# Moving the first heads' preparations earlier, and an HBM ring 256 KB further on

## The chip, the cores and the metric

The kernel runs on 1 core of one Trainium2 chip. The metric is the device time of one execution in microseconds (us), lower is better. Unprofiled runs give the time; one profiled execution gives the trace.

## The reference

For x of shape (32, 512, 256) in float32 it computes

```python
xn  = _layernorm(x)
out = x + attention(xn) + expert_ffn(xn)
# attention, 16 heads of width 16, relative positions:
content_score = einsum('bhsp,bhtp->bhst', q + u, k)
pos_score     = _relative_shift(einsum('bhsp,htp->bhst', q + v, pos))
weights       = softmax((content_score + pos_score) / sqrt(P))
att           = einsum('bhst,bhtp->bhsp', weights, val) @ Wo + bo
# expert FFN: softmax gate over 8 experts, each expert takes its top k tokens, gelu(x @ w1) @ w2,
# results weighted by the gate and scattered back with add
```

## The kernel before, in words

Three phases follow one another: attention, expert FFN, and the sum with the output projection. The change touches the attention phase alone. Its two stages:

- **The batch loop** (`for b in range(B)`, B = 32, once on each engine). SP loads x of batch b + 4 (L300) once batch b is normalised, stores the normalised batch to `xn_d` (L304) and its transposed form to `xt_d` (L308). DVE computes `statistics(b + 1)` (L616, L619) and `normalise(b)` (L624, L630). TensorE transposes (`turn_batch`, L810) and multiplies by the gate weights (`score(b - 1)`, L819). ACT takes square roots (`find_root`, L479) and evacuates the transposes (`copy_turned`, L486). The order on each engine is the order in which the code is written: each engine runs its own list and meets the others at semaphores.
- **The head loop** (512 heads: 16 turns of `body(i)` with 32 heads each). A head's position scores are made by TensorE (`position`, L907), evacuated by ACT to `xo` (L537), written by SP into one of 8 slots of the ring `xs_d` in HBM (L348, rows of 513 values), and read back one value shifted (L356, rows of 512), which is the relative shift. DVE adds content scores and the shifted scores (L677), ACT takes the exponential (L542), TensorE transposes the weights (L940), DVE and ACT evacuate them (L687, L551), and TensorE multiplies by the values (L956).

Before the head loop can start, the first heads need preparations: GpSimd splits the transposed batch 0 in high and low parts (`split_xt`, L447, L449, after SP's `load_xt(0)`, L313), TensorE projects values, queries and keys (`project_v` L863, `project_q` and `project_k` L846, all into the one PSUM bank `mp`), DVE evacuates the values (`stage_v`, L665), ACT the queries and keys (`keep_queries` L501, `keep_keys` L508), GpSimd splits them (`with_v`, `keys`, `with_u`; L417, L419, L437, L439), and TensorE spreads the queries over partitions (`spread_qv`, L830, L831), which DVE evacuates (`qv_evacuate`, L643). In the kernel before, these steps stand in the turns for batches 27 to 30 of the batch loop and right behind it, and the engine that takes a product out of `mp` does so in the same turn in which TensorE makes it. The ring is allocated as

```python
xs_d = nc.dram_tensor("xs_d", [8, S * (S + 1)], F32).ap()
```

so one slot is 512 x 513 x 4 = 1,050,624 bytes.

Of the kernel before, what the change touches and what calls it, by code (L numbers as in the profile page):

```python
# [9 lines left out]
F32 = mybir.dt.float32  # L10
# [5 lines left out]
P = 128  # L16
D = 256
DC = D // P
B = 32
S = 512  # L20
# [86 lines left out]
def attention_phase(nc, x, gate_w, w, consts, xn_d, xt_d, xs_d, att_d, sums_d, picks, chosen):  # L107
# [17 lines left out]
    with ExitStack() as ctx:  # L125
# [103 lines left out]
        k_kept = m.sem("k_kept")  # L229
# [9 lines left out]
        qv_out = m.sem("qv_out")  # L239
# [55 lines left out]
        with nc.Block() as block:  # L295

            @block.sync
            def _(sp):
                def load_x(b):
                    sp.dma_start(xin[:, b % NS], x[b].rearrange("(p t) d -> p t d", t=TT)).then_inc(x_in[b % NS], 16)  # L300
# [30 lines left out]
                for b in range(B):  # L331
                    store_xn(b)
                    if b + NS < B:
                        load_x(b + NS)
                    if b:
                        store_xt(b - 1)
                    if b == B - 8:
                        sp.wait_ge(xt_stored[0], 16)
                        load_xt(0)
                store_xt(B - 1)  # L340
# [133 lines left out]
            def _(act):  # L474
# [35 lines left out]
                for b in range(B):  # L510
                    find_root(b)
                    if b:
                        copy_turned(b - 1)
                    if b == 3:
                        act.wait_ge(const_in, 16 * CONST_LOADS)
                    if b in (3, 4):
                        keep_positions(b - 3)
                    if b == 5:
                        act.activation(wqkv[:, 0], wst[:, 0:3], ACT.Copy).then_inc(w_high, 1)
                    if 6 <= b < 6 + NG8 // 2:  # L520
                        g = 2 * (b - 6) + 1
                        act.wait_ge(p_spread, g + 1)
                        act.activation(pos[:, g], op[:, :], ACT.Copy).then_inc(p_out_act, 1)
                    if b == B - 3:
                        act.wait_ge(biased, 2)
                        keep_queries(0, 0)
                    if b == B - 2:
                        keep_keys(0, 0)
                copy_turned(B - 1)

# [77 lines left out]
            def _(dve):  # L608
# [29 lines left out]
                def qv_evacuate(i, g):  # L638
                    v = i * GROUPS + g
                    dve.wait_ge(qv_full, v + 1)  # L640

                    wait(dve, x_full, (v - 1) * GH * 2)
                    dve.tensor_copy(qv[:, g % 2], mp[:, :]).then_inc(qv_out, 1)  # L643
# [15 lines left out]
                def stage_v(i, bb, half):  # L659

                    b = i * 2 + bb
                    dve.wait_ge(v_full, b * 2 + half + 1)

                    wait(dve, o_full, (b - 1) * H)
                    dve.tensor_tensor(val[:, bb % 2, 2 * half:2 * half + 2, :, 0:HD],  # L665
                                      mp[:, :].rearrange("p (t h v) -> p t h v", t=2, h=H),
                                      bv[:, :].rearrange("p (h v) -> p h v", h=H).unsqueeze(1).to_broadcast([P, 2, H, HD]),
                                      ALU.add).then_inc(v_ready, 1)
# [46 lines left out]
                for b in range(B):  # L715
                    if b + 1 < B:
                        statistics(b + 1)
                    normalise(b)
                    if b == 2:
                        dve.wait_ge(const_in, 16 * CONST_LOADS)  # L720
                        for k in range(2):
                            dve.tensor_tensor(bias_q[:, k], vectors[:, 0], vectors[:, 3 + k], ALU.add).then_inc(biased, 1)
                    if b in (4, 5):
                        position_lows(b - 4)
                    if b == 6:
                        dve.wait_ge(w_high, 1)
                        dve.tensor_tensor(wqkv[:, 1], wst[:, 0:3], wqkv[:, 0].bitcast(F32), ALU.subtract).then_inc(w_low, 1)
                    if 7 <= b < 7 + NG8 // 2:
                        g = 2 * (b - 7)
                        dve.wait_ge(p_spread, g + 1)  # L730
                        dve.tensor_copy(pos[:, g], mp[:, :]).then_inc(p_out_dve, 1)
                    if b == B - 5:
                        dve.wait_ge(ones_set, 2)
                        stage_v(0, 0, 0)
                    if b == B - 4:
                        stage_v(0, 0, 1)

                qv_evacuate(0, 0)
                qv_evacuate(0, 1)
                qv_evacuate(0, 2)  # L740
                qv_evacuate(0, 3)
                kd_evacuate(0, 0)
# [60 lines left out]
            def _(pe):  # L803
# [9 lines left out]
                def score(b):  # L813

                    pe.wait_ge(copied, b + 1)
                    group, v = b // 4, b % 4
                    of_group = slice(group % 4 * PACK, (group % 4 + 1) * PACK)
                    for c in range(DC):
                        ins = pe.matmul(tp[of_group, group // 4, :], gw[:, c, PACK - NE - v * NE:2 * PACK - NE - v * NE],  # L819
                                        xts[:, b % NS, c, :], start=(v == 0 and c == 0), stop=(v == 3 and c == DC - 1))  # L820
                    ins.then_inc(scored, 1)
# [32 lines left out]
                def project_k(i, t):  # L854
                    project(1, t, k_full)
# [11 lines left out]
                def spread_qv(i, g):  # L867
                    v = i * TILES + g // (MH // GH)
                    pe.wait_ge(qv_high, v + 1)
                    pe.wait_ge(qv_low, v + 1)  # L870
                    spread_out(mp[:, :], QUERIES, g, qc[:, 1, 0], qc[:, 1, 1]).then_inc(qv_full, 1)
# [89 lines left out]
                for b in range(B):  # L961
                    turn_batch(b)
                    if b:
                        score(b - 1)
                    if b == 2:
                        pe.wait_ge(const_in, 16 * CONST_LOADS)
                    if b in (2, 3):
                        project_positions(b - 2)
                    if 6 <= b < 6 + NG8 // 2:
                        pe.wait_ge(p_low, DC)  # L970
                        spread_positions(2 * (b - 6))
                        spread_positions(2 * (b - 6) + 1)
                    if b == B - 5:
                        pe.wait_ge(w_low, 1)
                        pe.wait_ge(xt_low, 1)
                        pe.wait_ge(p_out_dve, NG8 // 2)
                        project_v(0, 0, 0)
                    if b == B - 4:
                        pe.wait_ge(v_ready, 1)
                        project_v(0, 0, 1)  # L980
                    if b == B - 3:
                        pe.wait_ge(v_ready, 2)
                        project_q(0, 0)
                    if b == B - 2:
                        pe.wait_ge(q_kept, 2)
                        project_k(0, 0)
                score(B - 1)
                pe.wait_ge(k_kept, 1)
                spread_qv(0, 0)
                pe.wait_ge(qv_out, 1)  # L990
                spread_qv(0, 1)
                pe.wait_ge(copied, B)
                for k in range(2):
                    for t in range(TT):
# [451 lines left out]
def build(nc, x, Wq, bq, Wk, bk, Wv, bv, Wp, bp, Wo, bo, u, v, gate_w, w1, w2, out):  # L1446
    names = ("sinusoid", "ident", "first_row", "spread")
    c = {n: nc.inline_tensor(a, name=f"const_{n}").ap() for n, a in zip(names, shape_constants())}
    xn_d = nc.dram_tensor("xn_d", [B * S, D], F32).ap()
    xt_d = nc.dram_tensor("xt_d", [B, P, DC, S], F32).ap()  # L1450
    ffn_d = nc.dram_tensor("ffn_d", [B * S, D], F32).ap()
    xs_d = nc.dram_tensor("xs_d", [8, S * (S + 1)], F32).ap()
    att_d = nc.dram_tensor("att_d", [B, D, S], F32).ap()
    sums_d = nc.dram_tensor("sums_d", [B, H, S], F32).ap()
    inv_d = nc.dram_tensor("inv_d", [B, H, S], F32).ap()
    weights = {"Wq": Wq, "Wk": Wk, "Wv": Wv, "Wp": Wp, "bq": bq, "bk": bk, "bv": bv, "bp": bp,
               "u": u.rearrange("a h b p -> (a h b p)"), "v": v.rearrange("a h b p -> (a h b p)")}
    with nc.sbuf_tensor("picks", [P, B * NE], U32) as picks, nc.sbuf_tensor("chosen", [P, B * NE], F32) as chosen:
        attention_phase(nc, x, gate_w, weights, (c["sinusoid"], c["ident"], c["first_row"], c["spread"]), xn_d, xt_d, xs_d,
                        att_d, sums_d, picks, chosen)  # L1460
        ffn_phase(nc, w1, w2, c["ident"], xn_d, picks, chosen, ffn_d, sums_d, inv_d)
    combine_phase(nc, x, Wo, bo, ffn_d, att_d, inv_d, out)
# [27 lines left out]
```

## Time and profile before

| what | value |
|---|---|
| time, median of 3 runs | 5658.08 us (5654.66 to 5665.97) |
| the profiled execution's own time | 5717.12 us |
| its span | 5715.3 us |
| mean granted TensorE clock | 0.936 of full speed |
| PE busy | 5210.5 us, 91% |
| DVE busy | 3630.7 us, 64% |
| ACT busy | 3470.4 us, 61% |
| POOL (GpSimd) busy | 1430.1 us, 25% |
| bytes moved | 1357.75 MB, mean 238 GB/s |

Busy times are sums over a span with different stages: the batch loop fills about the first 187 us, the head loop the time to about 3770 us, FFN and output the rest. PE is TensorE's multiplying, PEld its loading of weights, SP the engine that issues nearly all DMAs. "DMA share" is the mean busy share of the 16 DMA engines.

### The profile page before, as it was taken

The page shows a single profiled execution, that of the slowest core. Times are in us where ns is not written, and L with a number is a line of the kernel's source. Part 1 is how long each engine was busy: PE and PEld are TensorE (multiplying, and loading weights), DVE is VectorE, ACT ScalarE, POOL GpSimd, SP SyncE. Part 2 cuts the span into 40 slices and gives each one's busy share as a digit, 9 for nine tenths or more (in the row PEclk, how much of TensorE's full clock was granted, in tenths as well). Part 3 has the DMA queues.
Part 4 walks back from the last instruction along what each step waited for, and adds up shares of the span by engine and source line. Part 5 has one row for each costly group of instructions (what it writes and reads, how often), then busy time and mean ns, then how long its engine had stood idle before and what let it go on. Part 6 is the DMA issues. An engine that isn't in the chain of part 4 may idle for free. (4 is left out here: it accounts for less than half of the span.)

```text
span 5715.3 us, 126833 instructions
## 1 busy us (share of the span) xinstructions
PE 5210.5 (91%) x42412; PEld 3837.9 (67%) x42412; DVE 3630.7 (64%) x8008; ACT 3470.4 (61%) x5116; POOL 1430.1 (25%) x1032
## 2 busy tenths in 40 slices
PE   6799999999999899999999999979999999999755
PEld 2466666666666666666666666658888988888744
DVE  7598887787777777877777877854333333333233
ACT  2487777787787777777777877844443444344211
POOL 0111111111111111111111111114444444444355
PEclk9799999899899999999998999989999999999877
DMA  9799999999999999999999999983332233222398
GB/s 338 225 327 315 313 311 311 308 317 307 308 317 304 318 307 310 317 305 310 316 304 311 320 306 316 328 272 64 58 59 53 47 58 58 52 49 43 72 289 258
DMA packets 311142, 1357.75 MB, mean 238 GB/s; under 512 B 41792, under 2 KB 119360, under 8 KB 179136
## 3 DMA queue, kind: packets, MB, share of 16 engines
q1 hardware_dynamic: 256704, 1265.12, 69.5%
q0 software_dynamic: 49152, 67.14, 7.2%
q10 hardware_dynamic: 4608, 16.78, 0.8%
q8 instruction: 386, 6.32, 0.5%
q14 instruction: 292, 2.39, 0.1%
HBM read 691.42 MB, written 657.46 MB: 236 GB/s over the span
## 5 line engine op out<-in xcount | busy, mean ns | idle before, releaser
L677 DVE CUSTOM_DVE_ANT_0 att_shifted<-att_quad,att_shifted 128x512 f32<-128x512 f32 x2048 | 1345.4, 685 | 472.2 <-DMA att_shifted<-xs_d 295.2
L537 ACT ACTIVATE att_xo<-att_quad 128x1024 f32<-128x1024 f32 x1024 | 1049.2, 1025 | 720.5 <-PE att_quad L907 718.9
L542 ACT ACTIVATE att_shifted<-att_shifted,att_mn 128x512 f32<-128x512 f32 x2048 | 1359.1, 716 | 83.5 <-issue 75.7
L940 PE MATMUL att_tp<-att_ident,att_shifted 128*128 128x128 f32 x8192 | 1184.8, 290 | 1.0 <-DVE att_pt L687 0.4
L687 DVE COPY att_pt<-att_tp 128x512 f32<-128x512 f32 x1536 | 1014.6, 686 | 208.5 <-PE att_tp L940 207.9
L940 PEld LDWEIGHTS att_tp<-att_ident,att_shifted 128*128 128x128 f32 x8192 | 930.1, 147 | 316.3 <-issue 287.4
L919 PE MATMUL att_quad<-att_kd,att_qu 64*128 64x512 f32 x2048 | 827.5, 472 | 193.5 <-DVE att_mn L677 132.0
L1251 DVE TENSOR_TENSOR ffn_hp<-ffn_hf,ffn_hp 128x512 fp32r<-128x512 f32 x512 | 354.6, 693 | 925.7 <-ACT ffn_hf L1218 925.6
L907 PE MATMUL att_quad<-att_pos,att_qv 64*128 64x512 f32 x2048 | 907.0, 472 | 18.9 <-ACT att_xo L537 18.8
L1216 ACT ACTIVATE ffn_hp<-ffn_up 128x512 fp32r<-128x512 f32 x512 | 306.5, 599 | 926.5 <-PE ffn_up L1308 926.4
L1282 PE MATMUL ffn_yp<-ffn_w2p,ffn_hp 128*128 128x256 f32 x6144 | 831.0, 285 | 29.5 <-DVE ffn_w2p L1259 22.8
L1282 PEld LDWEIGHTS ffn_yp<-ffn_w2p,ffn_hp 128*128 128x128 f32 x6144 | 807.7, 193 | 70.1 <-issue 29.2
L1308 PE MATMUL ffn_up<-ffn_xp,ffn_w1p 128*128 128x512 f32 x3072 | 811.8, 401 | 33.4 <-DVE ffn_w1p L1246 33.4
L919 PEld LDWEIGHTS att_quad<-att_kd,att_qu 64*128 64x128 f32 x2048 | 333.8, 192 | 606.9 <-issue 381.6
L1308 PEld LDWEIGHTS ffn_up<-ffn_xp,ffn_w1p 128*128 128x128 f32 x3072 | 557.5, 194 | 128.4 <-issue 25.4
L1177 POOL DMA_INDIRECT ffn_d<-ffn_ys,picks x256 | 404.4, 1580 | 838.4 <-DVE ffn_ys L1240 824.7
L956 PE MATMUL att_op<-att_pt,att_val 128*17 128x128 f32 x16384 | 592.1, 289 | 0.2 <-issue 0.2
L956 PEld LDWEIGHTS att_op<-att_pt,att_val 128*17 128x17 f32 x16384 | 424.1, 102 | 188.9 <-issue 150.5
L437 POOL CAST att_kc<-att_qn 128x512 fp32r<-128x512 f32 x64 | 39.2, 612 | 1895.9 <-ACT att_qn L508 1895.9
L907 PEld LDWEIGHTS att_quad<-att_pos,att_qv 64*128 64x128 f32 x2048 | 368.4, 193 | 51.4 <-ACT att_xo L537 20.1
L417 POOL CAST att_qc<-att_qn 128x512 fp32r<-128x512 f32 x128 | 144.8, 1132 | 775.2 <-PE att_mp L831 702.6
L551 ACT ACTIVATE att_pt<-att_tp 128x512 f32<-128x512 f32 x512 | 306.3, 598 | 43.2 <-PE att_tp L940 41.7
(108 smaller groups left out, 4992.2 us busy)
## 6 DMA issues: line engine op xcount, KB each, us to landing
xs_d<-att_xo SPq DMA_DIRECT2D x512, 1026.0 KB, 12.1
att_shifted<-xs_d SPq DMA_DIRECT2D x512, 1024.0 KB, 8.9
att_shifted<-in_L_attn_x_dram SPq DMA_DIRECT2D x32, 512.0 KB, 7.5
xn_d<-att_shifted SPq DMA_DIRECT2D x32, 512.0 KB, 6.2
xt_d<-att_shifted SPq DMA_DIRECT2D x32, 512.0 KB, 7.4
att_xf<-xt_d SPq DMA_DIRECT2D x32, 512.0 KB, 9.9
att_d<-att_osb SPq DMA_DIRECT2D x512, 32.0 KB
ffn_d<-ffn_zero SPq DMA_DIRECT2D x8, 2048.0 KB, 24.8
```

The lines of the kernel that those rows point to most:

```text
L537: act.activation(xo[:, kk % NW, 2 * half:2 * half + 2, 1:S + 1], xp[:, :, :], ACT.Copy).then_inc(x_out, 1)
L542: act.activation(shifted[:, kk % NX, t], shifted[:, kk % NX, t], ACT.Exp, bias=mn[:, kk % NX, t:t + 1], scale=-1.0).then_inc(exp_done, 1)
L677: dve.tensor_tensor_reduce(out=shifted[:, kk % NX, t], in0=sp_[:, t % 2], in1=shifted[:, kk % NX, t], scale=-0.25, scalar=-NEG, op0=ALU.ad ...
L687: dve.tensor_copy(pt[:, t], tp[:, t % 2]).then_inc(t_out_dve, 1)
L907: ins = pe.matmul(xp[:, t % 2, :], qv[rows, kk // GH % 2, t * P:(t + 1) * P], pos[rows, kk // GH % NG8, :], start=True, stop=True)
L919: pe.matmul(sp_[:, t % 2, :], qu[rows, kk // GH % 2, t * P:(t + 1) * P], kd[rows, kk // GH % 2, :], start=True, stop=True).then_inc(s_full, 1)
L940: ins = pe.transpose(tp[:, c % 2, t * P:(t + 1) * P], shifted[:, kk % NX, t, c * P:(c + 1) * P], ident[:, :])
L956: ins = pe.matmul(op[32 * t:32 * t + HD + 1, kk % QH * P:(kk % QH + 1) * P], val[:, kk // H % 2, c, kk % H, :], pt[:, c, t * P:(t + 1) * P ...
L1177: pool.indirect_dma_start(ffn_d, bass.IndirectOffsetOnAxis(ap=picks[:, g * GB + k, e:e + 1], axis=0), ys[:, g % 2, k], None, compute_op=AL ...
L1251: dve.tensor_tensor(hp[:, g % 2, 1, f], hf[:, f % 2], hp[:, g % 2, 0, f].bitcast(F32), ALU.subtract).then_inc(h_low, 1)
L1282: ins = pe.matmul(yp[:, k % 2, 0:D], hp[:, g % 2, hi, f, k * CAP:(k + 1) * CAP], w2p[:, wi, f, :], start=(f == 0 and s == 0), stop=(f == F ...
L1308: ins = pe.matmul(up[:, f % 4, :], w1p[:, wi, c, f * P:(f + 1) * P], xp[:, g % 2, xi, c, :], start=(s == 0 and c == 0), stop=(s == 2 and c ...
```

## The change

The preparations of the first heads are spread over the turns 14 to 31 of the batch loop, three turns apart, and each consumer stands two turns behind the product it takes:

| step | turn before | turn now |
|---|---|---|
| `load_xt(0)` on SP | 24 | 8 |
| `project_v(0, 0, 0)` on TensorE, `stage_v(0, 0, 0)` on DVE | 27, 27 | 14, 16 |
| `project_v(0, 0, 1)`, `stage_v(0, 0, 1)` | 28, 28 | 17, 19 |
| `project_q(0, 0)`, `keep_queries(0, 0)` on ACT | 29, 29 | 20, 22 |
| `project_k(0, 0)`, `keep_keys(0, 0)` on ACT | 30, 30 | 23, 25 |
| `spread_qv(0, 0)`, `qv_evacuate(0, 0)` on DVE | behind the loop | 26, 28 |
| `spread_qv(0, 1)`, `qv_evacuate(0, 1)` | behind the loop | 29, 31 |

The ring `xs_d` begins 65,536 values (256 KB) further on, inside an allocation that is larger by as much. The slots' size and spacing stay.

```diff
@@ SP, batch loop
-                    if b == B - 8:
+                    if b == 8:
                         sp.wait_ge(xt_stored[0], 16)
                         load_xt(0)
@@ ACT, batch loop
-                    if b == B - 3:
+                    if b == 22:
                         act.wait_ge(biased, 2)
                         keep_queries(0, 0)
-                    if b == B - 2:
+                    if b == 25:
                         keep_keys(0, 0)
@@ DVE, batch loop
-                    if b == B - 5:
+                    if b == 16:
                         dve.wait_ge(ones_set, 2)
                         stage_v(0, 0, 0)
-                    if b == B - 4:
+                    if b == 19:
                         stage_v(0, 0, 1)
-
-                qv_evacuate(0, 0)
-                qv_evacuate(0, 1)
+                    if b == 28:
+                        qv_evacuate(0, 0)
+                    if b == 31:
+                        qv_evacuate(0, 1)
+
                 qv_evacuate(0, 2)
@@ TensorE, batch loop
-                    if b == B - 5:
+                    if b == 14:
                         pe.wait_ge(w_low, 1)
                         pe.wait_ge(xt_low, 1)
                         pe.wait_ge(p_out_dve, NG8 // 2)
                         project_v(0, 0, 0)
-                    if b == B - 4:
+                    if b == 17:
                         pe.wait_ge(v_ready, 1)
                         project_v(0, 0, 1)
-                    if b == B - 3:
+                    if b == 20:
                         pe.wait_ge(v_ready, 2)
                         project_q(0, 0)
-                    if b == B - 2:
+                    if b == 23:
                         pe.wait_ge(q_kept, 2)
                         project_k(0, 0)
+                    if b == 26:
+                        pe.wait_ge(k_kept, 1)
+                        spread_qv(0, 0)
+                    if b == 29:
+                        pe.wait_ge(qv_out, 1)
+                        spread_qv(0, 1)
                 score(B - 1)
-                pe.wait_ge(k_kept, 1)
-                spread_qv(0, 0)
-                pe.wait_ge(qv_out, 1)
-                spread_qv(0, 1)
                 pe.wait_ge(copied, B)
@@ HBM tensors
-    xs_d = nc.dram_tensor("xs_d", [8, S * (S + 1)], F32).ap()
+    xs_d = nc.dram_tensor("xs_d", [S * P + 8 * S * (S + 1)], F32).ap()[S * P:].rearrange("(k n) -> k n", k=8)
```

TensorE from the turn for batch 27 to the first position scores, before (L810 transposes a batch, L819 scores one, L863 and L846 are the projections, L830 and L831 the spreads, L907 the position scores):

```order
L863 MATMUL att_mp<-att_wqkv,att_xt 128x256 x12
L810 MATMUL att_quad<-att_ident,att_shifted 128x128 x8
L819 MATMUL att_tp<-att_shifted,att_osb 32x512 x2
L846 MATMUL att_mp<-att_xt,att_wqkv 128x512 x6
L810 MATMUL att_quad<-att_ident,att_shifted 128x128 x8
L819 MATMUL att_tp<-att_shifted,att_osb 32x512 x4
L830 MATMUL att_mp<-att_qc,att_spread 128x512
L831 MATMUL att_mp<-att_qc,att_spread 128x512
L830 MATMUL att_mp<-att_qc,att_spread 128x512
L831 MATMUL att_mp<-att_qc,att_spread 128x512
L907 MATMUL att_quad<-att_pos,att_qv 128x512 x8
```

The same engine now, from the turn for batch 29 on (the lines are two or four further down in the changed file):

```order
L821 MATMUL att_tp<-att_shifted,att_osb 32x512 x2
L832 MATMUL att_mp<-att_qc,att_spread 128x512
L833 MATMUL att_mp<-att_qc,att_spread 128x512
L812 MATMUL att_quad<-att_ident,att_shifted 128x128 x8
L821 MATMUL att_tp<-att_shifted,att_osb 32x512 x2
L812 MATMUL att_quad<-att_ident,att_shifted 128x128 x8
L821 MATMUL att_tp<-att_shifted,att_osb 32x512 x4
L909 MATMUL att_quad<-att_pos,att_qv 128x512 x8
```

The projections have left these turns, and between the last scores and the first position scores nothing is left on TensorE.

DVE at the end of the batch loop, before (L624, L630 normalise a batch, L616, L619 are its statistics, L665 takes the values out of `mp`, L643 the spread queries):

```order
L630 TENSOR_SCALAR att_shifted<-att_shifted,att_osb 128x256 x4
L665 TENSOR_TENSOR att_val<-att_mp,att_bv 128x32x16
L616 BN_STATS att_osb<-att_shifted 128x6 x4
L619 BN_AGGR att_osb<-att_osb 128x2 x4
L624 RECIPROCAL att_osb<-att_osb 128x4
L630 TENSOR_SCALAR att_shifted<-att_shifted,att_osb 128x256 x4
L643 CAST att_qv<-att_mp 128x512 x4
L657 CAST att_kd<-att_mp 128x512
```

DVE now, from the turn for batch 28 on:

```order
L630 TENSOR_SCALAR att_shifted<-att_shifted,att_osb 128x256 x4
L643 CAST att_qv<-att_mp 128x512
L616 BN_STATS att_osb<-att_shifted 128x6 x4
L619 BN_AGGR att_osb<-att_osb 128x2 x4
L624 RECIPROCAL att_osb<-att_osb 128x4
L630 TENSOR_SCALAR att_shifted<-att_shifted,att_osb 128x256 x4
L643 CAST att_qv<-att_mp 128x512 x3
L657 CAST att_kd<-att_mp 128x512
```

One of the four casts has moved ahead of three batches' normalisation, a second one directly behind the last; the L665 rows stand at batches 16 and 19 instead of 27 and 28.

## Rows read from the trace of the kernel before

**Rows 1.** Stretches: length; PE, PEld, DVE, ACT, POOL busy; clock; DMA share; GB/s.

```profile
80.20:128.25 48.05, 35.12 (x144) 14.57 (x144) 38.74 (x156) 15.86 (x24) 0.00 (x0) 1.00 1.02 409
128.25:179.57 51.32, 28.63 (x96) 13.15 (x96) 23.36 (x59) 7.82 (x12) 10.47 (x8) 0.82 0.39 152
189.00:229.00 40.00, 26.79 (x64) 13.72 (x63) 14.26 (x22) 16.98 (x18) 5.99 (x4) 0.58 0.83 249
250.00:450.00 200.00, 197.57 (x1975) 133.06 (x1973) 191.78 (x466) 169.36 (x244) 36.03 (x28) 1.00 1.00 324
1000.00:3000.00 2000.00, 1875.70 (x17662) 1261.50 (x17663) 1536.79 (x3597) 1525.27 (x2173) 319.98 (x250) 0.94 0.99 311
```

**Rows 2.** The page's GB/s in 40 equal slices of the span.

```profile
GB/s 338 225 327 315 313 311 311 308 317 307 308 317 304 318 307 310 317 305 310 316 304 311 320 306 316 328 272 64 58 59 53 47 58 58 52 49 43 72 289 258
```

**Rows 3.** Timeline of SP's queue: stores of batches 14, 26, 27, 28, 30 and 31.

```profile
80.20 0.32 SPq L304 DMA_DIRECT2D xn_d<-att_shifted  x1
...
128.25 0.32 SPq L304 DMA_DIRECT2D xn_d<-att_shifted  x1
...
135.14 0.32 SPq L304 DMA_DIRECT2D xn_d<-att_shifted  x1
...
146.38 0.32 SPq L304 DMA_DIRECT2D xn_d<-att_shifted  x1
...
167.80 0.32 SPq L304 DMA_DIRECT2D xn_d<-att_shifted  x1
...
179.57 0.32 SPq L304 DMA_DIRECT2D xn_d<-att_shifted  x1
```

**Rows 4.** Timeline of the turn for batch 28.

```profile
147.43 3.55 PE L819 MATMUL att_tp<-att_shifted,att_osb 128*32 128x512 f32 x4
147.54 1.02 ACT L486 ACTIVATE att_shifted<-att_quad 128x1024 f32<-128x1024 f32 x1 [2.34 <-PE att_quad L810]
...
150.91 1.70 PE L863 MATMUL att_mp<-att_wqkv,att_xt 128*128 128x256 f32 x12
152.65 0.69 DVE L665 TENSOR_TENSOR att_val<-att_mp,att_bv 128x512 f32<-128x512 f32 x1 [6.30 <-PE att_mp L863]
```

**Rows 5.** Timeline: DVE's normalisation with and without work on GpSimd.

```profile
126.84 1.38 DVE L630 TENSOR_SCALAR att_shifted<-att_shifted,att_osb 128x256 f32<-128x256 f32 x4
...
130.92 4.20 DVE L630 TENSOR_SCALAR att_shifted<-att_shifted,att_osb 128x256 f32<-128x256 f32 x4
131.49 1.06 POOL L447 CAST att_xt<-att_xf 128x1024 fp32r<-128x1024 f32 x1 [128.42 <-DMA att_xf<-xt_d]
132.63 2.34 POOL L449 TENSOR_TENSOR att_xt<-att_xf,att_xt 128x1024 fp32r<-128x1024 f32 x1
...
164.56 3.21 DVE L630 TENSOR_SCALAR att_shifted<-att_shifted,att_osb 128x256 f32<-128x256 f32 x4
...
175.14 4.41 DVE L630 TENSOR_SCALAR att_shifted<-att_shifted,att_osb 128x256 f32<-128x256 f32 x4
```

**Rows 6.** Timeline: a turn at the full clock, and the end of the batch loop.

```profile
120.31 1.09 PE L810 MATMUL att_quad<-att_ident,att_shifted 128*128 128x128 f32 x8 [1.05 <-DVE att_shifted L630]
...
121.33 1.90 PE L819 MATMUL att_tp<-att_shifted,att_osb 128*32 128x512 f32 x4
...
179.60 1.97 PE L810 MATMUL att_quad<-att_ident,att_shifted 128*128 128x128 f32 x8 [5.62 <-DVE att_shifted L630]
...
181.50 5.39 PE L819 MATMUL att_tp<-att_shifted,att_osb 128*32 128x512 f32 x8
...
187.58 0.69 DVE L643 CAST att_qv<-att_mp 128x512 fp32r<-128x512 f32 x1 [8.04 <-PE att_mp L831]
...
188.99 0.73 PE L907 MATMUL att_quad<-att_pos,att_qv 64*128 64x512 f32 x2
```

**Rows 7.** Waits of DVE from 84 to 130 us: total, times, longest.

```profile
DVE att_osb L616 <- DMA att_shifted<-in_L_attn_x_dram: 8.3, 12, 1.3
```

**Rows 8.** The ring's reads: count, duration min/median/max ns, first and last start us.

```profile
L356 SPq DMA_DIRECT2D att_shifted<-xs_d x512: 319/320/2119, 197.8 to 3761.0; - x171
```

## The prediction

> **What bounds the kernel now.** I read the stretches of the span first, then the timeline where they change. In the head loop the DMA engines are busy all the time, 0.99 of 2000 us, and move 311 GB/s [rows 1]; TensorE, with 1876 of 2000 us, follows close behind, and nothing on the other engines is above 77%. So that loop takes the time in which its bytes move, wherever it begins. In the batch loop between batches 14 and 26 the DMA engines are the bound too, at 1.02 and 409 GB/s: 12 batches in 48.05 us, 4.00 us each [rows 1, 3]. DVE is busy 38.74 us of these 48.05 and waits 8.3 us for loads of x [rows 1, 7]. From batch 27 on this breaks. The five batches 27 to 31 take 51.32 us, with the DMA share at 0.39 and 152 GB/s [rows 1, 3]. The turn for batch 28 shows why: DVE waits 6.30 us for the product that TensorE makes in the same turn, behind that batch's own transposes and scores [rows 4]. All engines stand in one chain there, from normalisation over transposes, scores and projection to the evacuation, and only then the next statistics. TensorE idles in it, its granted clock is 0.82 in this stretch (a mix of 2.4 and 1.2 GHz) and the same scores take 3.55 us instead of 1.90 [rows 1, 4, 6]. Behind the batch loop, two spreads with an evacuation between them stand ahead of the first position scores, which start at 188.99 [rows 6].
>
> **The change part by part.** The sum is made against the profiled execution, 5717.12 us, and is a difference that I then take from the median of the runs, 5658.08 us; the profiled execution is 1% above it.
>
> *Batches 27 to 31.* With each consumer two turns behind its product, no engine waits in its own turn for the others: when DVE reaches batch 16, TensorE made that product in turn 14. The chain of five turns goes, and the DMA engines bound these batches as they did the earlier ones. Five batches at 4.00 us make 20.0 us instead of 51.32: **-31.3 us**. A second way to the same number: 152 GB/s over 51.32 us are 7.8 MB, which at 409 GB/s take 19.1 us. These two lie close, so I take the first.
>
> *The load of batch 0's transposed form* (0.5 MB) leaves the stretch that is bound by DMA, where it takes 0.52 MB / 409 GB/s = 1.3 us, for turn 8, when the engines still have room: **-1.3 us**.
>
> *GpSimd's splits.* They read and write SBUF beside DVE's normalisation. Four tensor_scalars take 1.38 us alone and 4.20, 3.21 and 4.41 us with GpSimd at work [rows 5], so 2.8, 1.8 and 3.0 us more. The first of these comes with the split of batch 0, which now falls in turns 9 to 11, right behind the position spreads, where turns are a chain and DMA has slack: it costs between 0 (if it hits DVE while that waits) and 2.8 us; I take the middle, **+1.4 us**. The other two now fall in turns 22 to 26. There they meet DVE's wait for loads, 8.3 us, and with the two evacuations of the values (0.69 us each, rows 4) add 1.4 + 1.8 + 3.0 = 6.2 us, which is less. I cost them at nothing; that cover is gone if the loads should come faster. The two evacuations in turns 28 and 31 (0.69 us each) lie under loads and are the same work as before behind the loop.
>
> *TensorE's added work* in turns 14 to 29 is one step in three turns, at most 1.7 us [rows 4]; in 4.00 us TensorE is busy 35.12 / 12 = 2.9 us [rows 1]. A turn with 4.6 us is 0.6 us late and recovers in the next. Stores of the transposed batches, queued behind it on SP, shift by as much; four batches of x in flight cover this. Nothing.
>
> *Behind the batch loop.* From the last normalisation to the first position scores there were 188.99 - 179.57 = 9.4 us [rows 3, 6]. What stays is one batch's transposes and two batches' scores: 1.09 + 2 x 1.90 = 4.9 us at the full clock, which I expect because TensorE stays as busy as from 80 to 128 us; with the lead-in 5.2: **-4.2 us**. If the clock is low as before, 1.97 + 5.39 = 7.4 us [rows 6], and the gain is 2.0.
>
> *The ramp to the head loop* (189 to 229 us, clock 0.58 [rows 1]) keeps its steps. With a better clock it could give up to 5 us; I take 0.
>
> *The ring, 256 KB further on.* No instruction and no byte is changed, only addresses in HBM, those of the tensors that are allocated behind the ring included. The trace of before has no run with other addresses, so this is bounded by rows. Gain: the head loop ran at 324 GB/s from 250 to 450 us, with TensorE busy 197.57 of 200 us [rows 1], so 324 in place of 311 over the 3530 us from 229 us to the last read of the ring at 3761 [rows 8] is the most that TensorE leaves, -142 us. Loss: the slowest slice within the loop has 304 GB/s [rows 2], and a loop that is always as slow takes 311 / 304, +81 us. Inside these bounds I take **0**: the ring's eight slots already lie 1,050,624 bytes apart over 8.4 MB, the loop walks through all of them, and the rates of the slices scatter by a few per cent with no trend. A shift by a quarter of a slot leaves the distance between the slot that is written and the slot that is read as it was.
>
> Sum: -31.3 - 1.3 + 1.4 - 4.2 = -35.4 us, and the idle share of the DMA engines allows it: from 128.25 to 179.57 they stood still for 0.61 x 51.32 = 31 us. 5717 - 35 = 5682 us for a profiled execution, **5622.7 us** for the runs.
>
> **The rivals.**
>
> *1. GpSimd holds DVE up for the whole of its splits.* For: each of the three collisions in rows 5 cost nearly the length of the GpSimd work beside it (3.4 us of splits, 2.8 us lost). In the changed kernel the splits of queries and keys run beside batches that DMA feeds every 4.00 us, and if two collisions fall together the loads of x run late. Then 1.4 us more at turns 9 to 11 and up to 6.2 us in turns 16 to 26 are lost: 5622.7 + 7.6 = 5630 us. Against: DVE has 8.3 us of waits there. The Trainium skill has a rule for it, SBUF — State Buffer, section "Who interferes with whom": GpSimd and DVE share one port pair, tensor_scalar can take it, and whichever comes second is blocked until the first has finished, not slowed down. Rows 5 agree with that in kind (4.20 against 1.38 us), and by the rule alone this rival's time would come out.
>
> *2. The ring's new place is worse (the other side).* Mechanism: the write of one slot and the read of the one before meet at addresses that slow each other more, and each of 512 heads waits longer for its slot. For: at the same DMA share the batch loop moves 409 GB/s and the head loop 311 [rows 1], so packets do take longer there, and I can't say from which cause. It decides from the point where the loop loses more than 35.4 of 3530 us, that is below 311 x (1 - 0.01) = 308 GB/s. At the slowest slice's 304 GB/s: 5622.7 + 81 = 5704 us.
>
> *3. The ring's new place is better.* The same mechanism with the other sign. At 318 GB/s, which the better slices have [rows 2]: 3530 x (1 - 311 / 318) = -78, 5545 us.
>
> *4. The batch loop's gain is not passed on.* The head loop starts earlier, but its first 220 us run at 324 GB/s, above the mean, and if that is a lead gathered before, which an earlier start would lose, the end stays: about 5658 us. Against: the DMA engines are full from about 200 us on, and the bytes are the same.
>
> **How the numbers follow.** About 0.2%, 11 us, is what a measurement of this kernel can tell from no change. Forecast 0.64 (its own range 5608 to 5638), rival 1 0.10, rival 2 0.10, rival 3 0.10, rival 4 0.06. Faster: 0.64 + 0.10 + 0.10 = 0.84. Same: 0.06. Slower: 0.10. For 8 in 10 the range takes forecast and rival 1, and the milder halves of 2 and 3 (a ring that moves the loop by 1% either way, 35 us): 5585 to 5650 us.
>
> **What would show it.** Right: the stores of batches 27 to 31 about 4 us apart, at a DMA share near 1; DVE without waits for TensorE's products in L665; the first position scores near 153 us instead of 189; and from 1000 to 3000 us still 311 GB/s and 0.94. Wrong: normalisations of over 4 us in several turns (rival 1); a head loop at another rate, with the prologue as forecast (rivals 2 and 3); a prologue that is 35 us shorter with an end that is not (rival 4).

## The result, and the profile after

| | before | changed |
|---|---|---|
| time, median of 4 runs | 5660.73 us (5654.66 to 5665.97) | 5417.08 us (5408.59 to 5427.88) |
| the profiled execution's span | 5715.3 us | 5407.3 us |
| mean granted clock | 0.936 | 0.96 |

The ratio is 0.9571, 95% interval 0.9546 to 0.9595: 244 us faster, where 35 us were forecast. The span fell by 308 us; the profiled execution of before lies 1% above its own runs and that of after does not, so the ratio of the runs is the measure, and the traces only say where.

The page's GB/s line and its two ring issues, after (KB each, median us from issue to landing):

```profile
GB/s 346 314 341 335 330 338 341 334 343 336 339 338 330 338 342 330 332 344 333 334 343 334 336 341 353 276 169 58 52 52 58 50 53 56 60 43 44 80 305 263
...
xs_d<-att_xo SPq DMA_DIRECT2D x512, 1026.0 KB, 10.4
att_shifted<-xs_d SPq DMA_DIRECT2D x512, 1024.0 KB, 8.5
```

Before, the same two issues took longer, the write above all:

```profile
xs_d<-att_xo SPq DMA_DIRECT2D x512, 1026.0 KB, 12.1
att_shifted<-xs_d SPq DMA_DIRECT2D x512, 1024.0 KB, 8.9
```

Stretches after (columns as in [rows 1]): the batch loop from batch 14 on, the ramp, the start of the head loop, and its middle:

```profile
80.20:144.61 64.41, 54.12 (x234) 25.16 (x234) 56.33 (x217) 22.64 (x36) 7.27 (x6) 1.00 1.02 398
150.80:190.60 39.80, 26.60 (x62) 13.56 (x61) 13.35 (x20) 16.44 (x18) 5.96 (x4) 0.55 0.73 252
...
200.00:400.00 200.00, 198.97 (x1941) 134.33 (x1940) 190.97 (x462) 166.96 (x239) 35.92 (x28) 0.98 0.97 339
...
1000.00:2000.00 1000.00, 966.85 (x9568) 655.54 (x9560) 830.69 (x1950) 823.25 (x1177) 175.02 (x136) 0.98 0.98 337
```

The whole head loop of each, first before, from the end of the ramp to the ring's last read:

```profile
229.00:3761.00 3532.00, 3332.96 (x31424) 2236.63 (x31422) 2795.12 (x6579) 2715.53 (x3869) 557.08 (x436) 0.94 0.99 313
```

```profile
190.60:3461.80 3271.20, 3187.76 (x31380) 2158.53 (x31380) 2782.90 (x6573) 2702.91 (x3865) 558.03 (x436) 0.98 0.98 338
```

It is 261 us shorter in the traces, with the same share of busy DMA engines and the same bytes, at 338 instead of 313 GB/s. The stretch ahead of it is 38 us shorter, all that follows 9 us.

The batch loop did what was forecast. SP's stores of batches 14, 26, 27, 30 and 31 after, then the end of the loop on the other engines:

```profile
79.03 0.32 SPq L304 DMA_DIRECT2D xn_d<-att_shifted  x1
...
128.44 0.32 SPq L304 DMA_DIRECT2D xn_d<-att_shifted  x1
...
131.64 0.52 SPq L304 DMA_DIRECT2D xn_d<-att_shifted  x1
...
143.10 0.32 SPq L304 DMA_DIRECT2D xn_d<-att_shifted  x1
...
144.61 0.48 SPq L304 DMA_DIRECT2D xn_d<-att_shifted  x1
```

```profile
87.08 0.68 DVE L665 TENSOR_TENSOR att_val<-att_mp,att_bv 128x512 f32<-128x512 f32 x1
...
121.98 2.69 DVE L630 TENSOR_SCALAR att_shifted<-att_shifted,att_osb 128x256 f32<-128x256 f32 x4
122.49 0.69 POOL L437 CAST att_kc<-att_qn 128x512 fp32r<-128x512 f32 x1 [8.35 <-ACT att_qn L508]
...
147.01 3.62 PE L821 MATMUL att_tp<-att_shifted,att_osb 128*32 128x512 f32 x8
...
150.56 0.72 PE L909 MATMUL att_quad<-att_pos,att_qv 64*128 64x512 f32 x2
```

Batches 27 to 31 take 144.61 - 128.44 = 16.2 us instead of 51.32 [rows 3]. L665 waits for nothing, where it waited 6.30 us [rows 4]. Two normalisations beside GpSimd's splits take 2.69 us and, at 126.50, 1.91 us instead of 1.38. The last two batches' scores take 3.62 us for eight matmuls instead of 5.39 [rows 6].

### The profile page after: what moved, and what is told of

Same layout as the page of the kernel before. It is cut to its first block and busy times, and to the rows that moved or that the text cites. A ratio compares the mean times of both kernels' runs of the same rounds, so it can differ in the third digit from the quotient of the medians.

```text
span 5407.3 us, 126833 instructions
## 1 busy us (share of the span) xinstructions
PE 5052.8 (93%) x42412; PEld 3753.5 (69%) x42412; DVE 3619.1 (67%) x8008; ACT 3459.4 (64%) x5116; POOL 1429.7 (26%) x1032
## 3 DMA queue, kind: packets, MB, share of 16 engines
q14 instruction: 292, 2.39, 0.1%
## 5 line engine op out<-in xcount | busy, mean ns | idle before, releaser
L677 DVE CUSTOM_DVE_ANT_0 att_shifted<-att_quad,att_shifted 128x512 f32<-128x512 f32 x2048 | 1330.3, 683 | 248.5 <-PE att_quad L921 162.5
L942 PE MATMUL att_tp<-att_ident,att_shifted 128*128 128x128 f32 x8192 | 1142.5, 283 | 0.9 <-ACT att_shifted L542 0.4
L942 PEld LDWEIGHTS att_tp<-att_ident,att_shifted 128*128 128x128 f32 x8192 | 894.9, 143 | 304.7 <-issue 281.8
L909 PE MATMUL att_quad<-att_pos,att_qv 64*128 64x512 f32 x2048 | 852.8, 455 | 17.4 <-ACT att_xo L537 17.4
L921 PE MATMUL att_quad<-att_kd,att_qu 64*128 64x512 f32 x2048 | 775.1, 455 | 78.5 <-issue 49.6
L921 PEld LDWEIGHTS att_quad<-att_kd,att_qu 64*128 64x128 f32 x2048 | 317.4, 188 | 441.2 <-issue 360.3
L958 PE MATMUL att_op<-att_pt,att_val 128*17 128x128 f32 x16384 | 564.4, 280 | 0.2 <-issue 0.2
L958 PEld LDWEIGHTS att_op<-att_pt,att_val 128*17 128x17 f32 x16384 | 410.8, 99 | 191.8 <-issue 151.4
L909 PEld LDWEIGHTS att_quad<-att_pos,att_qv 64*128 64x128 f32 x2048 | 349.8, 189 | 48.9 <-ACT att_xo L537 18.3
L1170 POOL DMA_INDIRECT ffn_xg<-xn_d,picks x256 | 280.3, 1095 | 154.6 <-issue 75.6
## 6 DMA issues: line engine op xcount, KB each, us to landing
xs_d<-att_xo SPq DMA_DIRECT2D x512, 1026.0 KB, 10.4
```

The lines of the kernel that those rows point to most:

```text
L677: dve.tensor_tensor_reduce(out=shifted[:, kk % NX, t], in0=sp_[:, t % 2], in1=shifted[:, kk % NX, t], scale=-0.25, scalar=-NEG, op0=ALU.ad ...
L909: ins = pe.matmul(xp[:, t % 2, :], qv[rows, kk // GH % 2, t * P:(t + 1) * P], pos[rows, kk // GH % NG8, :], start=True, stop=True)
L921: pe.matmul(sp_[:, t % 2, :], qu[rows, kk // GH % 2, t * P:(t + 1) * P], kd[rows, kk // GH % 2, :], start=True, stop=True).then_inc(s_full, 1)
L942: ins = pe.transpose(tp[:, c % 2, t * P:(t + 1) * P], shifted[:, kk % NX, t, c * P:(c + 1) * P], ident[:, :])
L958: ins = pe.matmul(op[32 * t:32 * t + HD + 1, kk % QH * P:(kk % QH + 1) * P], val[:, kk // H % 2, c, kk % H, :], pt[:, c, t * P:(t + 1) * P ...
```

## The experiments

All ratios are to the kernel before, run on the same chip beside the kernel in question. The experiments ran on four chips, on which the kernel before takes 5623 to 5755 us, so kernels of different chips are compared through the ratios. The first three experiments take the change apart. "Preparations alone" is the base for the ring experiments behind them.

**ring_only.** The kernel before with one line of the change:

```diff
-    xs_d = nc.dram_tensor("xs_d", [8, S * (S + 1)], F32).ap()
+    xs_d = nc.dram_tensor("xs_d", [S * P + 8 * S * (S + 1)], F32).ap()[S * P:].rearrange("(k n) -> k n", k=8)
```

> The kernel before with the ring alone 256 KB further on. Theory A (the ring's place sets the rate of the head loop): about 210 us under the kernel before, near 5450 us, 336 GB/s from 1000 to 3000 us as in the changed kernel instead of 311. Theory B (the place does nothing, and the earlier start changes how the head loop runs, through the clock or the order of the transfers): within 15 us of the kernel before, 5650 us, at 311 GB/s.

Measured: 0.9635 (0.9603 to 0.9668), 5450.48 us.

**preps_only.** The changed kernel with that line put back.

> The changed kernel with the ring where it was. Theory A: the first ring write near 154 us as in the changed kernel, and about 35 us under the kernel before, near 5623 us, with 311 GB/s in the head loop. Theory B: all of the change's gain, near 5417 us, and 336 GB/s.

Measured: 0.9947 (0.9931 to 0.9963), 5627.54 us. The two parts add up: -3.65% and -0.53% are -4.18%, the change gives -4.29%. The middle of the head loop, of ring_only and then of preps_only:

```profile
1000.00:3000.00 2000.00, 1943.79 (x19097) 1318.35 (x19096) 1657.59 (x3889) 1643.19 (x2350) 346.34 (x270) 0.97 0.98 336
```

```profile
1000.00:3000.00 2000.00, 1882.03 (x17984) 1267.75 (x17983) 1562.32 (x3662) 1551.34 (x2212) 322.40 (x252) 0.95 0.99 316
```

Theory A holds: the ring's place sets the rate, whatever the batch loop does. The preparations are worth 30 us (21 to 39) of the 5659 us.

**pad_behind.** The same allocation, with the slack at its end:

```diff
-...ap()[S * P:].rearrange("(k n) -> k n", k=8)
+...ap()[:8 * S * (S + 1)].rearrange("(k n) -> k n", k=8)
```

> The changed kernel with the 256 KB behind the ring instead of ahead of it: the ring stands where it was, the tensors behind it (attention output, sums, inverses) stand where the changed kernel has them. If the place of the ring itself counts: about 5623 us, as with the preparations alone. If it is the distance to those other tensors: about 5417 us, as the changed kernel.

Measured: 0.9949 (0.9928 to 0.9969). It is the ring's own place, not that of the tensors behind it.

**Other places.** Only the number in that line differs: `2 * S * P` for 512 KB, `S * P // 4` for 64 KB, `4 * S * P` for 1 MB, `3 * S * P` for 768 KB, `3 * S * P // 2` for 384 KB, `6 * S * P` for 1536 KB.

> The changed kernel with the ring 512 KB further on instead of 256 KB. If any place other than the old one is free of a conflict: about 5417 us. If the address counts by a bit that 256 KB turns and 512 KB does not: about 5623 us, at 311 GB/s. If it counts in steps (the amount matters): another time than both.

> The changed kernel with the ring 64 KB further on instead of 256 KB. If what counts is a coarse address bit at 256 KB or above: 5627 us, as without a shift. [...] If the gain grows with the shift: near 5575 us, a quarter of 210 us.

> The changed kernel with the ring 1 MB further on. Each slot then lies 2 KB from where the next slot was. If the gain is a matter of an address bit at 256 or 512 KB, which 1 MB leaves as it was: near 5627 us. If the old place alone is bad, or the gain grows with the shift and then stays: 5417 us or less.

> The changed kernel with the ring 768 KB further on. So far, as ratios to the kernel before: 0 and 64 KB 0.995 and 0.997, 256 KB 0.957, 512 KB 0.953, 1 MB 0.991. [...]

> The changed kernel with the ring 384 KB further on, between the two best places so far. If the time is a smooth curve of the place with its lowest point between 256 and 512 KB: 0.950 or a little less. If it goes by single bits: anything up to 0.995.

> The changed kernel with the ring 1.5 MB further on. If the effect repeats every 1 MB, as 1 MB = 0.991 beside 0.995 for none suggests: as 512 KB, 0.953. If the place counts by a longer pattern, or only the surroundings of the old start: anything else, 0.99 if no better than 1 MB.

| ring further on by | ratio (95% interval) | GB/s, 1000 to 3000 us | write to landing, median us |
|---|---|---|---|
| 0 (preparations alone) | 0.9947 (0.9931 to 0.9963) | 316 | 11.7 |
| 64 KB | 0.9969 (0.9956 to 0.9981) | 316 | 11.8 |
| 256 KB (the change) | 0.9571 (0.9546 to 0.9595) | 336 | 10.4 |
| 384 KB | 0.9876 (0.9833 to 0.9919) | 309 | 12.3 |
| 512 KB | 0.9531 (0.9500 to 0.9563) | 340 | 10.2 |
| 768 KB | 0.9850 (0.9823 to 0.9876) | 319 | 11.6 |
| 1 MB | 0.9908 (0.9883 to 0.9933) | 319 | 11.6 |
| 1536 KB | 0.9464 (0.9432 to 0.9496) | 331 | 10.8 |

The 384 and 1536 KB rows are from a chip on which the kernel before takes 5755 us, so their GB/s compare with each other only. 384 KB was run on that chip alone, so that the order of places is the same on every chip is not shown for it; for the old place three chips agree (0.9947 here, 0.9948 and 0.9925 below), for 512 KB two (0.9531 here, 0.9519 below). The curve isn't smooth (384 KB between two good places is poor), which rules out a gain that grows with the shift. A pattern that mirrors about 512 KB falls too: 768 KB would then be as 256 KB, 0.957, and it is 0.9850. The totals suggest a repeat of about 1 MB: 1 MB is near none, and 1536 KB is at least as good as 512 KB. The rule for the amounts between stays open. That 512 KB (5386.5 us) beats the change itself is likely from the medians, but the two intervals overlap and they were not run side by side.

**wide_slots.** Each slot gets 256 KB of slack behind it, the ring begins at its old place: `xs_d = ...[8, S * (S + 1) + S * P]...[:, :S * (S + 1)]`.

> The preparations alone, the ring begins where it was, each slot 256 KB further from the one before (slot k moves by k x 256 KB). If the absolute place counts by an address bit at 256 KB: slots 1, 3, 5, 7 turn and 0, 2, 4, 6 turn only by higher bits, so about half of the ring's gain, near 5520 us. If the spacing of the slots counts: another time altogether, the full gain or a loss. If only a fixed stretch of memory at the ring's old start is slow: slot 0 alone stays slow, near 5440 us.

Measured: 0.9698 (0.9666 to 0.9730), 5445.48 us on a chip with 5622.93 before, which is 5488 us for 5659 before. That lies between the forecasts of 5520 and 5440, and the total alone doesn't decide. The records of the DMA packets say more. Mean duration of the 8208-byte write packets of each slot, worked out from the trace's packet records by the order in which they start, 128 per write (64 writes per slot; the standard error of a mean is about 3 ns, and the same slot differs by up to 12 ns between kernels with the preparations moved and the writes at the old place). The last two rows are from one chip: the writes at the old place, and the ring moved as a whole by 768 KB:

```
slot                       0    1    2    3    4    5    6    7
preps_only, ns           379  399  373  370  374  385  374  373
wide_slots, ns           380  373  331  349  372  376  334  353
 its slot moved by, KB     0  256  512  768 1024 1280 1536 1792
read_xn_0, ns            375  392  378  369  368  384  371  373
shift_768k, ns           352  389  342  348  374  385  362  360
```

In wide_slots the slot that is moved by 1 MB is as slow as the one not moved, and those moved by 512 and 1536 KB are both some 40 ns faster. So the place counts slot by slot, and these slots fit a repeat of 1 MB. But that can't be the whole pattern. In shift_768k all slots move alike and stand about 1 MB apart, and yet slots 0 and 2 are 22 and 20 ns faster than 4 and 6, which read_xn_0 doesn't have. In shift_384k, too, slots 0, 2 and 3 are 20 to 26 ns faster than 4, 6 and 7. The poor totals of these two rings may thus be those of rings of which only a part stands at a better place.

**perm3.** The slots used in another order, at the old place: `xs_d[slot * 3 % 8]` in place of `xs_d[slot]` in the write and the read.

> The preparations alone, the ring where it was, its eight slots used in the order 0, 3, 6, 1, 4, 7, 2, 5: slots in use at the same time lie 3 MB apart or 5 MB, no longer 1 MB. If the distance between the slot written and the slot read sets the rate: clearly under 5627 us, toward 5417. If the absolute place of each slot does: 5627 us within 20 us.

Measured: 0.9948 (0.9929 to 0.9968), as the preparations alone with 0.9947. The distance between the slot written and the slot read doesn't count, at this place at least.

**Reads and writes apart.** Base is the preparations alone. The reads take xn_d (written in the batch loop, ordinary numbers) instead of the ring:

```diff
-    sp.dma_start(shifted[:, slot], xs_d[slot][S:S + S * S]...)
+    sp.dma_start(shifted[:, slot], xn_d.rearrange("a b -> (a b)")[off + slot * S * (S + 1) + S:...]...)
```

with `off` 0, then `2 * S * P` (512 KB), then 0 again with the ring, that is the writes, 512 KB further on.

> The preparations alone, the ring where it was, but the read-back of each head takes the same 1 MB pieces, at the same spacing, from the start of xn_d instead of the ring (what is left out: the relative shift, the position scores don't reach the result). If the slow rate comes from reading at a place that lies like the ring's to the blocks of 1 MB: about as the preparations alone, 0.995. If it comes from reading what lies near the rows just written: clearly faster, toward 0.957.

> As the kernel that reads from xn_d, but from 512 KB behind its start; the writes stay where they were (the position scores don't reach the result here either). If the reads' place sets the rate: most of the 4.2% of the 512 KB ring, near 0.96, against the same kernel at 0 KB. If the writes' place does: no change against it, 0.995.

> Writes to the ring 512 KB further on, reads from the start of xn_d (the position scores don't reach the result). If the writes' place sets the rate: near 0.955. If the reads' place alone: as with both at 0, 0.995. If both count, as the packets' mean times suggest (reads 445 to 390 ns, writes 381 to 366 ns between before and the changed kernel): a smaller part of the gain, near 0.985.

Measured: 0.9925 (0.9908 to 0.9941), 0.9902 (0.9872 to 0.9933), 0.9519 (0.9502 to 0.9537). Reading a tensor that nobody writes at the time gains nothing clear over the 0.9947 of the preparations alone, so the slow rate doesn't come from reading what was just written. The place of the reads is worth nothing clear, at the two places tried; the place of the writes gives the whole gain of the 512 KB ring. Write and read issues of read_xn_512k, then of write_512k_read_xn_0:

```profile
xs_d<-att_xo SPq DMA_DIRECT2D x512, 1026.0 KB, 11.7
att_shifted<-xn_d SPq DMA_DIRECT2D x512, 1024.0 KB, 8.8
```

```profile
xs_d<-att_xo SPq DMA_DIRECT2D x512, 1026.0 KB, 9.8
att_shifted<-xn_d SPq DMA_DIRECT2D x512, 1024.0 KB, 8.5
```

**Even rows.** Is the odd row of 513 values, 8208 bytes per partition, part of it? Writes of 8192 bytes per partition, and reads from the slot's start:

```diff
-    sp.dma_start(xs_d[slot].rearrange("(p t c) -> p t c", t=TT, c=S + 1), xo[:, kk % NW])
+    sp.dma_start(xs_d[slot][:P * TT * S].rearrange("(p n) -> p n", p=P), xo[:, kk % NW].rearrange("p t c -> p (t c)")[:, :TT * S])
-    sp.dma_start(shifted[:, slot], xs_d[slot][S:S + S * S]...)
+    sp.dma_start(shifted[:, slot], xs_d[slot][:S * S]...)
```

> The preparations alone, ring where it was, but each write takes the first 8192 bytes of a partition to rows of 8192 bytes (what is left out: the last 4 of 2052 values of each partition and the relative shift). If the slow place needs the odd rows of 8208 bytes: fast here without any shift, near 0.955 of the kernel before. If it does not: near 0.995, and the same with 512 KB further on is near 0.955.

> As the kernel with even rows, with the ring 512 KB further on (the same is left out). If odd rows are needed for the slow place: equal to the one at 0 KB within 0.5%. If not: 4% under it, near 0.955.

Measured: 0.9253 (0.9219 to 0.9288) with the ring at its old place, 0.9272 (0.9240 to 0.9304) at 512 KB. With even rows these two places make no difference, and both kernels are faster than any odd-row kernel (the best, 1536 KB, had 0.9464 on the same chip). The issues and the middle of the loop of even_rows_0:

```profile
xs_d<-att_xo SPq DMA_DIRECT2D x512, 1024.0 KB, 6.1
att_shifted<-xs_d SPq DMA_DIRECT2D x512, 1024.0 KB, 8.4
```

```profile
1000.00:3000.00 2000.00, 1971.12 (x19733) 1340.83 (x19732) 1707.69 (x4021) 1696.20 (x2428) 359.65 (x280) 0.99 0.93 347
```

The write lands in 6.1 us (5.9 at 512 KB), where preps_only, on another chip, has 11.7. The DMA engines are no longer full (0.93), so the loop has another bound there; TensorE, busy for 1971 of 2000 us at a clock of 0.99, is the nearest. A bound elsewhere could hide an effect of the place in the total, but the landing times show none either. The edit drops 4 of 2052 values of a partition, 0.2% of the bytes, which can't be the cause. It changes the length of a row and the rows' alignment together, and it starts the reads 2 KB earlier; the runs don't separate these.

## Why the prediction was right or wrong

**Right, by its own steps:** the bound and the preparations. Forecast -35.4 us, measured by preps_only -30 us (-39 to -21). In the traces the first position scores come 188.99 - 150.56 = 38.4 us earlier; whether a few us of that are lost again behind them can't be told from these intervals. The sum is nearly right, in part by luck, since its terms are off either way:

- *Batches 27 to 31*: forecast 20.0 us instead of 51.32, measured 16.2. The DMA engines were full, as forecast, but moved only 390 GB/s x 16.17 us = 6.3 MB there, where the prediction counted 7.8 MB. They stay full behind the last normalisation (0.99 of the time from 144.61 to 150.56 us), so a part of the last batches' bytes goes out under TensorE's last scores. The 12 batches ahead took 128.44 - 79.03 = 49.4 us instead of 48.05, so the -1.3 us for the moved load don't show there; that the added work took them is likely, but not shown.
- *GpSimd's splits*: 1.4 us at turns 9 to 11 forecast. The step from batch 9 to batch 10 did take 65.61 - 56.56 = 9.0 us instead of 7.5, but not through GpSimd: its split ran from 57.03 to 60.48 us, between two normalisations that both took 1.38 us. It was TensorE, whose four scores of that turn took 3.62 us at a granted clock of 0.50 instead of 2.39 us at 0.79:

```profile
55.16 1.38 DVE L630 TENSOR_SCALAR att_shifted<-att_shifted,att_osb 128x256 f32<-128x256 f32 x4
...
58.14 2.34 POOL L449 TENSOR_TENSOR att_xt<-att_xf,att_xt 128x1024 fp32r<-128x1024 f32 x1
...
58.49 3.62 PE L821 MATMUL att_tp<-att_shifted,att_osb 128*32 128x512 f32 x4
...
64.20 1.38 DVE L630 TENSOR_SCALAR att_shifted<-att_shifted,att_osb 128x256 f32<-128x256 f32 x4
```

  In the kernel before, the same turn has this row:

```profile
61.19 2.39 PE L819 MATMUL att_tp<-att_shifted,att_osb 128*32 128x512 f32 x4
```

  So this term was 0, and the 1.5 us that seem to match it are chance: preps_only, with the same split in the same turn, takes 61.92 - 54.37 = 7.55 us for that step, with scores of 2.44 us. The two later collisions happened, smaller than priced: 2.69 and 1.91 us instead of 1.38, 1.8 us lost where 4.8 were counted, and the statistics behind them found their loads landed, so these waits hid it. Rival 1 did not come about. By the port rule that I had cited from the Trainium skill, SBUF — State Buffer, section "Who interferes with whom", a block needs the two to overlap. The trace agrees: `with_v` at 111.4 to 114.1 us overlapped a normalisation for its last 0.3 us only, and that took 1.40 us.
- *Behind the batch loop*: forecast 5.2 us from the last normalisation to the first position scores, measured 150.56 - 144.61 = 6.0.

**Wrong: the ring.** The step that failed is "Inside these bounds I take 0: the ring's eight slots already lie 1,050,624 bytes apart [...] A shift by a quarter of a slot leaves the distance between the slot that is written and the slot that is read as it was." Two things were wrong in it. The distance doesn't count (perm3, and the reads from xn_d); the place of the written rows does, and it is worth 3.65% alone (ring_only), where the term had 0. And eight slots were no sample of places: in preps_only their write packets take 370 to 399 ns, the second and the sixth in order of use the longest, and perm3 has the same two on top with other slots, so the order of use makes that spread and not the place. If the effect repeats about every 1 MB, as the experiments suggest, all eight stand at nearly the same place in that pattern, and the old ring showed none of the better ones. I read the missing spread between slots as evidence for no effect, and it was none.

**Wrong too: the bound of the gain.** I let the head loop gain at most 142 us, because TensorE was busy for 197.57 of 200 us at 324 GB/s [rows 1]. After the change it is busy 198.97 of 200 at 339 GB/s, and with even rows the loop runs at 347. What was wrong is the unit. By matmuls, 1975 in 200 us are 9.9 per us, and the middle of the loop had 17662 in 2000 us, 8.8 [rows 1]. Even rows come to 9.9 per us as well, at 347 GB/s. So the pace of that stretch may well be TensorE's limit, but it carried fewer bytes per matmul than the middle does, and its GB/s priced it too low: by matmuls the bound is 3530 x (1 - 8.83 / 9.875) = 373 us, not 142. (Some matmul records can be missing; ACT's counts give the same ratio within 1%.) So rival 3, which had the right mechanism and sign, was priced too small (-78 us, where ring_only shows -3.65%, some 207 us), and the range ended above the measured time.

The clue that stood in the rows and that I did weigh, but too lightly: at a full DMA share the batch loop moved 409 GB/s and the head loop 311 [rows 1]. A full share only says that packets were in flight. Between 1000 and 3000 us, from the packet records (writes or reads of the ring alone: at least 14 of that kind in flight and under 2 of the other; both: at least 2 of each; GB/s of all packets):

```
                      before                 changed
writes alone    17% of the time, 373 GB/s    24%, 374 GB/s
reads alone     18%, 296 GB/s                24%, 349 GB/s
both            56%, 300 GB/s                43%, 322 GB/s
```

Writes alone run at the same rate; with the better place there is less time with both in flight, and that time and the reads alone run faster. Why, these records don't show. The Trainium skill says in HBM Reference, section "Specifications (TRN2)", that a core streaming alone is held by its 16 DMA engines, near 425 GB/s. The batch loop comes close to that; the head loop does not, with the same engines full, and its rate moves with the address of the writes.

**Open.** Which part of the memory or of the DMA path is met by odd rows at the bad places is not shown. Shown is: the place of the writes, not that of the reads; with rows of 8208 bytes and, at the two places tried, not with 8192; and slot by slot. A repeat of about 1 MB fits the totals and most slots, but not the slots of shift_768k, which differ at equal shifts. No theory here gives the order in between (384 and 768 KB poor, 256 and 512 KB good).

## What to carry to other kernels

A loop at a full DMA share but well under the rate that another stage of the same kernel reaches may have room left: compare GB/s at equal share, and try the place and the row length of the HBM buffer it writes, by one line. When only one place was ever run, a change of place has an unknown price, here up to some 5%, and the slots of one ring at a stride of about 1 MB are a poor sample of places. Price the ceiling that another engine sets in that engine's own work per us, not in GB/s of a short stretch. A term that comes out right is checked on the rows it was said to come from. Work that is spread over a pipelined loop with its consumer two turns behind the producer cost almost nothing here, and broke up the chain that it had made over five turns, with both in the same turn.

## What the runs showed of the hardware that I had not expected

- The place of a written HBM buffer, with nothing else changed, moved the whole kernel between 0.997 and 0.946 of the kernel before (on different chips).
- Writes of 128 rows of 8208 bytes at the old place took 11.7 us from issue to landing (preps_only), writes of 8192 bytes 6.1 us (even_rows_0), in loops otherwise nearly alike.
- Slots of one ring, all moved by 768 KB, did not fare alike: write packets took 352 and 342 ns in slots 0 and 2, 374 and 362 ns in slots 4 and 6 (shift_768k).
- The clock follows: granted 0.944 with the preparations alone, 0.96 with the change, 0.967 with even rows, though no matmul was changed. From 1000 to 3000 us TensorE is busy for 1882 us in the first and 1971 us in the last, so it has fewer gaps, and less time passes at the lower of its two levels.
